# First cross attention: q and k in two 12-bit parts, four products laid over a head's 32 rows, scores in one float32r pass

## The chip, the cores and the metric

The program runs on one core of a Trainium2 chip. TensorE (PE) multiplies matrices and writes only to PSUM; VectorE (DVE), ScalarE (ACT) and GpSimd (POOL) do the elementwise work; SyncE (SP) issues nearly all DMA transfers. The engines run side by side and meet at semaphores. The metric is the device time of one execution in microseconds: the median of three runs of the kernel before is 2702.38 (2698.11 to 2705.56).

## The reference, cut to what matters

Six layers follow each other, each `x = layernorm(x + f(x))`: windowed self attention, cross attention, a mixture of experts, causal self attention, a second cross attention and a ternary feed forward. The change is in the second of them. 64 sequences of 128 tokens of width 128 are handled one by one there:

```
q = (x1 @ Wq + bq)                      # 16 heads of 8 columns
k = concat([x2 @ Wk + bk, memory_k])    # 128 keys from fside, 120 from ctx
v = concat([x2 @ Wv + bv, memory_v])
attn = softmax(einsum('bhqd,bhkd->bhqk', q, k) * D ** -0.5)
out = einsum('bhqk,bhkd->bhqd', attn, v) @ Wp + bp
```

with `x1` the stream, `x2 = fside_BxSxS_0`, and `memory_k = memory_v = ctx_1024`. All of it is float32.

## The kernel before, in words

`attend_keys_major` is the stage. Five engine programs run the same software pipeline, `pipeline(eng, step, ring, nseq, ...)`: `step(c)` is written for a counter c and touches several sequences at different ages (`a = c + 2`, `b = c + 1`, `m = c - 1`, ...), four buffers deep (ring 4); `need(eng, sem, value)` is a wait. The order on each engine is the order in which `step` is written; the middle of the stage is a loop of four steps. There are no planner and no priorities.

A sequence goes this way. SP loads x, ctx and the transposed fside and ctx. TensorE transposes x and projects q, k and v (L1560 to L1562). ScalarE copies q, scaled and with its bias, into `qT` and k into `xf` behind the ctx columns (L1587, L1589), so that the 248 keys of a head lie together. Heads have 8 rows each. The 128 rows of q and k hold 16 heads: 4 row groups of 32 rows, 4 heads in each. GpSimd makes `Qm` (L1732), q four times side by side with all but one head's rows of each 32 set to zero, so that one product over 32 rows gives one head.

Scores are computed twice. "Across" (L1478, L1489), queries on the partitions, 128 x 248 per head, two heads to a PSUM tile, gives VectorE the row maxima (`maxima`, L1625). "Down" (L1473), keys on the partitions, 120 or 128 keys x 4 heads x 128 queries, gets the negated maxima added by a bfloat16 product (L1485, `NB`) and is what ScalarE exponentiates (`exps`, L1577). `scores(c, r)` is one of four rounds of a step: two row groups' down products of an older sequence, mixed with the two other row groups' across products of sequence c. Between the rounds stand `weigh` (L1504, exponents times values), the transposes and the projections. A float32 product appears in the trace as two records, a bfloat16 one as one.

The maxima are split into three bfloat16 parts by GpSimd (L1719 to L1727), turned by TensorE (L1523), and copied by VectorE (L1665). VectorE also does the softmax division, the value bias, and most of the layer norm.

SP's step has seven transfers (L1432, L1433, L1436, L1440, L1444, L1448, L1449), 60 or 64 KB each. They wait for what frees a buffer.

Of the kernel before, what the change touches and what calls it, by code (L numbers as in the profile page):

```python
# [16 lines left out]
F32 = mybir.dt.float32  # L17
BF16 = mybir.dt.bfloat16
U32 = mybir.dt.uint32
# [21 lines left out]
BLANKS = 8  # L41

# [93 lines left out]
def allocate(K):  # L136
# [8 lines left out]
    K.alibi = K.sb("alibi", [P, WH * 48])  # L145
# [7 lines left out]
    K.blank = K.sb("blank", [P, BLANKS, ROW])  # L153
    K.half = K.sb("half", [P, 2])
    K.eps = K.sb("eps", [P, 1])
    K.Mself = K.sb("Mself", [P, WH * P])
    K.Nself = K.sb("Nself", [P, WH * P])
    K.Gram = K.sb("Gram", [P, 2 * P])
# [14 lines left out]
    K.tstep = K.sb("tstep", [P, 3])  # L173

# [84 lines left out]
def late_loads(K, D):  # L259

    return [
        (K.xw[:, 0, :], D["L0_xattn_Wq"]), (K.xw[:, 1, :], D["L0_xattn_Wk"]),
        (K.xw[:, 2, :], D["L0_xattn_Wv"]), (K.xw[:, 3, :], D["L0_xattn_Wp"]),
        (K.xb[:, 0:1], D["L0_xattn_bq"].rearrange("(d a) -> d a", a=1)),
        (K.xb[:, 1:2], D["L0_xattn_bk"].rearrange("(d a) -> d a", a=1)),
# [19 lines left out]
def attend_window(K, D, tag, x_dram, out_dram, nseq):  # L285
# [14 lines left out]
    with ExitStack() as ctx:  # L300
# [53 lines left out]
        with nc.Block() as block:  # L354
            @block.sync
            def _(sp):
# [972 lines left out]
def attend_keys_major(K, D, tag, x_dram, routed, nseq):  # L1329
# [6 lines left out]
    places = (slice(0, CTX), slice(CTX, CTX + P))  # L1336
# [6 lines left out]
    with ExitStack() as ctx:  # L1343
# [3 lines left out]
        def sem(name):  # L1347
# [6 lines left out]
        xf = [sb(f"xf{i}", [P, 2 * P + CTX + P]) for i in range(ring)]  # L1354
        qT = [sb(f"qT{i}", [P, P]) for i in range(2)]
        Qm = [sb(f"Qm{i}", [P, J * P]) for i in range(ring)]
# [24 lines left out]
        f_in = [sem(f"f_in{i}") for i in range(ring)]  # L1381
        xT_out = [sem(f"xT_out{i}") for i in range(ring)]
# [7 lines left out]
        cleared, ready, masked, put_ctx, split, maxed = (sem(n) for n in (  # L1390
            "cleared", "ready", "masked", "put_ctx", "split", "maxed"))
# [6 lines left out]
        cT, kT = slice(2 * P, 2 * P + CTX), slice(2 * P + CTX, 2 * P + CTX + P)  # L1398
        every = slice(2 * P, 2 * P + CTX + P)
# [24 lines left out]
        with nc.Block() as block:  # L1424
            @block.sync
            def _(sp):
                def step(c):
                    a, l, s, o = c + 4, c + 3, c, c - 5
                    if a.live:
                        need(sp, in_sb, (a - 4).done())  # L1430
                        need(sp, put_ctx, (a - 4).done())
                        sp.dma_start(x[a.slot][:], x_dram[a.n]).then_inc(x_in[a.slot], 16)  # L1432
                        sp.dma_start(cx[a.slot][0:CTX, :], D["ctx_1024"][a.n]).then_inc(x_in[a.slot], 16)  # L1433
                    if s.live:
# [21 lines left out]
            def _(pe):  # L1456
# [3 lines left out]
                def scores(c, r):  # L1460
                    t, k, ck, tg, sg, j0 = round_of(c, r)
                    size = sizes[ck]
                    if c.live and r == 0:
                        need(pe, masked, c.done())
                        need(pe, qk_sb, c.done(2))
                    for n in range(2):
                        h = 2 * r + n
                        g, to = tg[n], T[turn[h]]
                        if t.live:
# [3 lines left out]
                            pe.matmul(to[0:size, :], xf[t.slot][rows(g), every][:, places[ck]], Qm[t.slot][rows(g), :],  # L1473
                                      start=True, stop=False)
                        g, to = sg[n], S[turn[h]]
                        if c.live:
                            need(pe, maxed, (c if before[h] < h else c - 1).done(2 * R, before[h] + 1))
                            pe.matmul(to[:, 0:CTX + P], Qm[c.slot][rows(g), P * j0:P * j0 + P],  # L1478
                                      xf[c.slot][rows(g), every], start=True, stop=True)
                    for n in range(2):  # L1480
                        h = 2 * r + n
                        g, to = tg[n], T[turn[h]]
                        if t.live:
                            need(pe, nb_sb, t.done())
# [767 lines left out]
```

## Time and profile before

| | us |
|---|---|
| median of 3 runs | 2702.38 |
| span of the profiled execution (it has no other time of its own) | 2695.8 |
| TensorE busy | 2502.7 (93%) |
| VectorE busy | 1849.6 (69%) |
| ScalarE busy | 1737.7 (64%) |
| GpSimd busy | 1401.1 (52%) |
| first cross attention, its first DMA to its last | 477.84 to about 1124 |
| granted TensorE clock, mean | 0.967 |

The span runs from the first to the last instruction. Busy time is the time in which an engine has at least one instruction in progress; register, semaphore and DMA-issuing instructions do not count. SPq is SP's queue of transfers: its rows give the moment and the length of an issue, not of the transfer. In the waits, an engine's line is followed by what ended its idle time. PEld is the loading of weights, which overlaps with PE.

### The profile page before, as it was taken

The numbers are of one execution on the slowest core, as the hardware profiler recorded it, in microseconds if no ns is written. First come the engines' busy times: TensorE is split into PE (matmuls) and PEld (weight loads), VectorE is DVE, ScalarE is ACT, GpSimd is POOL, SyncE is SP. The second block draws the span as 40 slices with busy tenths as digits, with TensorE's granted clock in tenths as the row PEclk, the third lists the DMA queues.
The fourth block names the chain that finished last, engine by engine and source line by source line (L and its number), as shares of the span: only waits on it lengthen the run. The fifth ranks groups of instructions, "written<-read, shape, count | busy, mean of one in ns | idle before, by whom it ended". The sixth has DMA issues, their size and how long they took to land. (4 is left out here: it accounts for less than half of the span.)

```text
span 2695.8 us, 95989 instructions
## 1 busy us (share of the span) xinstructions
PE 2502.7 (93%) x29950; PEld 2007.2 (74%) x29951; DVE 1849.6 (69%) x5434; ACT 1737.7 (64%) x6375; POOL 1401.1 (52%) x2914
## 2 busy tenths in 40 slices
PE   7999999799999999788889969999999799999995
PEld 6888888577777777487667758888888688888883
DVE  4565555588888888564334448888887388888886
ACT  4666666355555555213556638888888588888883
POOL 2333333233444344165774447777776266666664
PEclk9999999799999999899999979999999899999997
DMA  6332322211111111123332211111111111111100
GB/s 158 100 88 79 89 81 65 65 49 48 49 48 48 48 47 44 37 85 84 78 80 66 66 48 53 47 53 49 50 53 37 33 31 32 31 31 31 31 26 11
DMA packets 270161, 151.37 MB, mean 56 GB/s; under 512 B 51776, under 2 KB 263744, under 8 KB 270016
## 3 DMA queue, kind: packets, MB, share of 16 engines
q1 hardware_dynamic: 261312, 131.57, 18.2%
q0 software_dynamic: 8704, 17.97, 1.9%
q8 instruction: 78, 1.28, 0.2%
q14 instruction: 67, 0.55, 0.1%
HBM read 92.52 MB, written 48.51 MB: 52 GB/s over the span
## 5 line engine op out<-in xcount | busy, mean ns | idle before, releaser
L1187 ACT ACTIVATE pr<-psS,small 128x128 f32<-128x128 f32 x1024 | 366.7, 384 | 95.9 <-DVE small L1258 94.0
L1625 DVE TENSOR_REDUCE small<-psS 128x2 f32<-128x496 f32 x512 | 321.4, 669 | 90.3 <-PE psS L1489 89.1
L1577 ACT ACTIVATE pr<-psT 120x512 f32<-120x512 f32 (+1 forms) x384 | 215.1, 595 | 136.9 <-PE psT L1485 124.5
L1473 PE MATMUL psT<-cross_Qm,cross_xf 32*120 32x512 f32 (+1 forms) x768 | 292.1, 641 | 0.5 <-ACT pr L1577 0.2
L1187 ACT ACTIVATION_READ_ACCUMULATOR pr<-psS,small 128x1 f32 x1024 | 226.1, 221 | 0.0
L1478 PE MATMUL psS<-cross_xf,cross_Qm 32*128 32x248 f32 x1024 | 209.1, 428 | 1.1 <-DVE small L1625 1.1
L2172 POOL DMA_INDIRECT results<-experts_ob,experts_xb x144 | 138.5, 962 | 115.4 <-ACT experts_ob L1992 100.5
L1258 DVE TENSOR_REDUCE small<-psS 128x8 f32<-128x1024 f32 x128 | 156.7, 1224 | 60.5 <-PE psS L1152 60.3
L2112 DVE SCALAR_TENSOR_TENSOR experts_bgh<-experts_bth,psS 128x256 f32<-128x256 f32 x144 | 60.7, 421 | 198.9 <-ACT experts_bth L1984 198.9
L956 POOL TENSOR_SCALAR pr<-pr,small 128x120 f32<-128x120 f32 x512 | 180.4, 372 | 23.3 <-DVE small L910 23.3
L814 ACT ACTIVATE pr<-psS,small 128x120 f32<-128x120 f32 x512 | 179.0, 391 | 5.0 <-DVE small L929 5.0
L1489 PE MATMUL psS<-cross_xf,cross_Qm 32*128 32x248 f32 x1024 | 181.4, 376 | 0.0
L484 ACT ACTIVATE pr<-pr,small 128x48 f32<-128x48 f32 x512 | 166.9, 331 | 2.9 <-DVE small L551 2.9
L1111 PE MATMUL psT<-ident,pr 128*128 128x128 f32 x1024 | 161.6, 281 | 0.2
L1152 PEld LDWEIGHTS psS<-self_qk,self_Qm 32*128 32x128 f32 x2048 | 125.7, 188 | 45.9 <-issue 45.9
L2163 POOL DMA_INDIRECT slots<-routed_x,experts_idx x128 | 123.6, 965 | 66.7 <-issue 38.1
L470 ACT COPY self_Y<-psW 128x512 f32<-128x512 f32 x128 | 68.7, 589 | 126.8 <-PE psW L456 126.8
L1152 PE MATMUL psS<-self_qk,self_Qm 32*128 32x128 f32 x2048 | 150.3, 285 | 0.0
L1473 PE MATMUL psS<-cross_Qm,cross_xf 32*120 32x512 f32 (+1 forms) x256 | 143.9, 642 | 0.0
L1504 PEld LDWEIGHTS psW<-pr,cross_Vx 120*32 120x32 f32 (+1 forms) x4096 | 104.0, 109 | 52.7 <-issue 51.8
L583 POOL TENSOR_TENSOR small<-small,eps 128x1 f32<-128x1 f32 x64 | 12.2, 191 | 249.0 <-DVE small L517 249.0
L1577 ACT ACTIVATE pr<-psS 120x512 f32<-120x512 f32 (+1 forms) x128 | 76.1, 595 | 98.9 <-PE psT L1485 98.9
(323 smaller groups left out, 8058.1 us busy)
## 6 DMA issues: line engine op xcount, KB each, us to landing
self_parts<-results SPq DMA_DIRECT2D x64, 192.0 KB, 2.4
slots<-blank SPq DMA_DIRECT2D x18, 520.0 KB, 4.5
experts_xb<-slots SPq DMA_DIRECT2D x144, 65.0 KB, 1.9
self_near<-in_x SPq DMA_DIRECT2D x128, 64.0 KB, 1.9
between<-self_xo SPq DMA_DIRECT2D x128, 64.0 KB, 1.6
cross_x<-between SPq DMA_DIRECT2D x128, 64.0 KB, 1.8
cross_res<-between SPq DMA_DIRECT2D x128, 64.0 KB, 1.8
self_x<-in_x SPq DMA_DIRECT2D x64, 64.0 KB, 1.8
```

Source lines behind the costliest of these rows:

```text
L484: last = act.activation(head(pr[e.slot], h), head(pr[e.slot], h), ACT.Exp, bias=nmax[e.slot % 2][:, h:h + 1], accum_out=tot[e.slot][:, h:h ...
L814: last = act.activation(pr[b.slot][:, i * P:i * P + CTX], S0[:, i * P:i * P + CTX], ACT.Exp, bias=nmax[b.slot % 2][:, i:i + 1], accum_out= ...
L956: last = pool.tensor_scalar(pr[w.slot][:, i * P:i * P + CTX], pr[w.slot][:, i * P:i * P + CTX], inv[w.slot][:, i:i + 1], 1.0, ALU.mult, AL ...
L1111: last = pe.transpose(W[half][:, n * P:(n + 1) * P], pr[t.slot % 4][:, (4 * half + n) * P:(4 * half + n + 1) * P], K.ident[:])
L1152: last = pe.matmul(K.S[u.slot % 2][:, 512 * half + m * P:512 * half + (m + 1) * P], Qm[i.slot % 2][rows(g), m * P:(m + 1) * P], qk[i.slot] ...
L1187: last = act.activation(pr[e.slot % 4][:, cols], K.S[e.slot % 2][:, cols], ACT.Exp, bias=nmax[e.slot % 4][:, n:n + 1], accum_out=tot[k.slo ...
L1258: dve.tensor_reduce(nmax[u.slot % 4][:], src, AX.X, ALU.max, negate=True).then_inc(maxed, 1)
L1473: pe.matmul(to[0:size, :], xf[t.slot][rows(g), every][:, places[ck]], Qm[t.slot][rows(g), :], start=True, stop=False)
L1478: pe.matmul(to[:, 0:CTX + P], Qm[c.slot][rows(g), P * j0:P * j0 + P], xf[c.slot][rows(g), every], start=True, stop=True)
L1489: pe.matmul(to[:, 256:256 + CTX + P], Qm[c.slot][rows(g), P * j0 + P:P * j0 + 2 * P], xf[c.slot][rows(g), every], start=True, stop=True).t ...
L1577: act.activation(PT[k][0:sizes[ck], 512 * n:512 * n + 512], T[turn[2 * r + n]][0:sizes[ck], :], ACT.Exp).then_inc(exped, 1)
L1625: dve.tensor_reduce(nmax[c.slot % 2][:, J * sg[n] + j0:J * sg[n] + j0 + 2], src, AX.X, ALU.max, negate=True).then_inc(maxed, 1)
```

## The change

Both operands of a score are cut by bits. `high` is the value with its lower 12 bits cleared (VectorE, `bitwise_and` with `0xFFFFF000`), `low` is the value minus `high` (GpSimd); each fits in 12 bits. A score is then four products, high-high, high-low, low-high and low-low, and as a head has only 8 rows, these four take the 32 rows of a row group: row 4d + n of a group holds, for dimension d, product n's part. The two parts of q and k are stored in DRAM (`K.parts`) and loaded back in that layout (`pack`, four heads of 376 columns: 128 of queries, 128 of fside keys, 120 of ctx keys) by six DMAs. For that the columns of Wq, Wk, their biases and a copy of ctx are reordered once outside the kernel (`by_place`). The masked `Qm` goes. Scores are float32r products of `pack` with itself: the down product of 512 columns becomes four of 128, the across product stays at 248 columns. The stage's pipeline is one step longer: projections of q and k run at c + 3, parts are made and stored at c + 2, and `pack` is loaded at c + 1. The value product stays at its old age (now `h = c + 2` in TensorE's step, with its own semaphore `v_ps`), the fside load moves from c + 3 to c + 4.

Some buffers used only by the first stage are given back after it (`early`) to make room, and the first stage's SP now waits for the last blank stores into `slots` (`K.emptied`).

```diff
@@ SP, step of the first cross attention
-                    a, l, s, o = c + 4, c + 3, c, c - 5
+                    a, l, s, o, e, h = c + 4, c + 3, c, c - 5, c + 1, c + 2
+                    if e.live:
+                        need(sp, T_ps, (e - 4).done(2 * R))
+                        need(sp, parts_out[e.slot], e.p * 32 + 32)
+                        for n in range(4):
+                            to = pack[e.slot][n::4, :, :]
+                            of = K.parts[e.slot].rearrange("(j s) h n -> s j h n", j=J)
+                            if n // 2 == n % 2:
+                                sp.dma_start(to, of[:, :, n // 2, :]).then_inc(pack_in[e.slot], 16)
+                            else:
+                                sp.dma_start(to[:, :, queries], of[:, :, n // 2, queries]).then_inc(pack_in[e.slot], 16)
+                                sp.dma_start(to[:, :, keys], of[:, :, n % 2, keys]).then_inc(pack_in[e.slot], 16)
                     if a.live:
...
+                        need(sp, v_ps, (a - 4).done())
+                        sp.dma_start(xf[a.slot][:, P:2 * P], D["t_fside"][a.n]).then_inc(f_in[a.slot], 16)
+                    if l.live:
+                        need(sp, parts_out[(l - 2).slot], (l - 2).p * 32 + 32)
+                        sp.dma_start(low[l.slot % 2][:, 2 * P:], D["t_ctxq"][l.n]).then_inc(c_in[l.slot], 16)
...
-                    if l.live:
-                        need(sp, T_ps, (l - 4).done(2 * R, 4))
-                        sp.dma_start(xf[l.slot][:, P:2 * P], D["t_fside"][l.n]).then_inc(f_in[l.slot], 16)
-                        sp.dma_start(xf[l.slot][:, cT], D["t_ctx"][l.n]).then_inc(f_in[l.slot], 16)
+                    if h.live:
+                        need(sp, low_sb, h.done())
+                        sp.dma_start(K.parts[h.slot][:, 0, :], high[h.slot % 2][:]).then_inc(parts_out[h.slot], 16)
+                        sp.dma_start(K.parts[h.slot][:, 1, :], low[h.slot % 2][:]).then_inc(parts_out[h.slot], 16)
@@ TensorE, one round of scores
-                            pe.matmul(to[0:size, :], xf[t.slot][rows(g), every][:, places[ck]], Qm[t.slot][rows(g), :],
-                                      start=True, stop=False)
+                            pe.matmul(to[0:size, P * j:P * j + P], pack[t.slot][rows(g), j, places[ck]].bitcast(F32R),
+                                      pack[t.slot][rows(g), j, queries].bitcast(F32R), start=(j == 0), stop=False)
...
-                            pe.matmul(to[:, 0:CTX + P], Qm[c.slot][rows(g), P * j0:P * j0 + P],
-                                      xf[c.slot][rows(g), every], start=True, stop=True)
+                            last = pe.matmul(to[:, 256 * j:256 * j + CTX + P], pack[c.slot][rows(g), j0 + j, queries].bitcast(F32R),
+                                             pack[c.slot][rows(g), j0 + j, keys].bitcast(F32R), start=True, stop=True)
@@ TensorE, order in a round: down(j) and across(j) of both row groups
+                        down(n, 0)
...
+                        across(n, 0)
+                    down(0, 1)
+                    down(1, 1)
+                    across(0, 1)
+                    down(0, 2)
+                    down(1, 2)
+                    across(1, 1)
+                    down(0, 3)
+                    down(1, 3)
@@ VectorE, before the first maxima of a step
+                    if h.live:
+                        need(dve, qk_sb, h.done(2))
+                        need(dve, c_in[h.slot], h.landed())
+                        need(dve, parts_out[c.slot], c.p * 32 + 32)
+                        dve.tensor_scalar(high[h.slot % 2][:].bitcast(U32), low[h.slot % 2][:].bitcast(U32), UPPER, None,
+                                          ALU.bitwise_and).then_inc(top_sb, 1)
@@ GpSimd
-                        pool.tensor_tensor(Qm[b.slot][:].rearrange("p (j q) -> p j q", j=J),
-                                           qT[b.slot % 2][:].rearrange("p (j q) -> p j q", j=1).to_broadcast([P, J, P]),
-                                           K.quadmask[:].rearrange("p (j q) -> p j q", q=1).to_broadcast([P, J, P]),
-                                           ALU.mult).then_inc(masked, 1)
+                    if h.live:
+                        need(pool, top_sb, h.done())
+                        pool.tensor_tensor(low[h.slot % 2][:], low[h.slot % 2][:], high[h.slot % 2][:],
+                                           ALU.subtract).then_inc(low_sb, 1)
@@ the stage before, end of SP's program
+                sp.wait_ge(K.emptied, 16 * empty.shape[0])
```

SP's queue, a step of the kernel before, in the fill of the pipeline (the semaphores in brackets are what an instruction waits for):

```order
322 L1448 DMA cross0_xf0<-in_t_fside 128x128 [waits cross0_T_ps]
323 L1449 DMA cross0_xf0<-in_t_ctx 128x120
324 L1432 DMA cross0_x2<-between0 128x128 [waits cross0_put_ctx,cross0_in_sb]
325 L1433 DMA cross0_cx2<-in_ctx_1024 120x128
326 L1436 DMA cross0_res2<-between0 128x128 [waits cross0_joined]
327 L1440 DMA routed_xT<-cross0_xoT0 128x128 [waits cross0_turned_sb]
328 L1444 DMA routed_x<-cross0_xo1 128x128 [waits cross0_normed]
```

The same queue of the changed kernel, from the stores of one step to the middle of the next (`parts` is the DRAM buffer, `pack` the layout of 32-row groups, `high` and `low` the two parts):

```order
396 L1475 DMA parts<-cross0_high0 128x376 [waits cross0_low_sb]
397 L1476 DMA parts<-cross0_low0 128x376
398 L1447 DMA cross0_pack0<-parts 32x4x376 [waits cross0_parts_out0,cross0_T_ps]
399 L1449 DMA cross0_pack0<-parts 32x4x128
400 L1450 DMA cross0_pack0<-parts 32x4x248
401 L1449 DMA cross0_pack0<-parts 32x4x128
402 L1450 DMA cross0_pack0<-parts 32x4x248
403 L1447 DMA cross0_pack0<-parts 32x4x376
404 L1454 DMA cross0_x3<-between0 128x128 [waits cross0_put_ctx,cross0_in_sb]
405 L1455 DMA cross0_cx3<-in_ctx_1024 120x128
406 L1457 DMA cross0_xf3<-in_t_fside 128x128 [waits cross0_v_ps]
407 L1460 DMA cross0_low0<-in_t_ctxq 128x120 [waits cross0_parts_out0]
```

A step of SP goes from 7 transfers to 15: `res`, `routed_xT` and `routed_x` follow as before and then the next two stores. The load in row 398 waits for `parts_out0`, which the stores in rows 396 and 397 raise when they have landed.

TensorE, the last round of a step, before (`psT` and `psS` are the PSUM tiles, `Qm` the masked queries, `xf` the keys):

```order
729 L1473 MATMUL psT<-cross0_Qm2,cross0_xf2 120x512 [waits cross0_exped]
730 L1478 MATMUL psS<-cross0_xf3,cross0_Qm3 128x248 [waits cross0_maxed]
731 L1473 MATMUL psT<-cross0_Qm2,cross0_xf2 120x512 [waits cross0_exped]
732 L1478 MATMUL psS<-cross0_xf3,cross0_Qm3 128x248 [waits cross0_maxed]
733 L1485 MATMUL psT<-cross0_NB0,cross0_onesb 120x512 [waits cross0_nb_sb]
734 L1489 MATMUL psS<-cross0_xf3,cross0_Qm3 128x248
735 L1485 MATMUL psT<-cross0_NB0,cross0_onesb 120x512 [waits cross0_nb_sb]
736 L1489 MATMUL psS<-cross0_xf3,cross0_Qm3 128x248
```

The same round of the changed kernel:

```order
694 L1496 MATMUL psT<-cross0_pack1 120x128 [waits cross0_exped]
695 L1502 MATMUL psS<-cross0_pack2 128x248 [waits cross0_maxed]
696 L1496 MATMUL psT<-cross0_pack1 120x128 [waits cross0_exped]
697 L1502 MATMUL psS<-cross0_pack2 128x248 [waits cross0_maxed]
698 L1496 MATMUL psT<-cross0_pack1 120x128 x2
699 L1502 MATMUL psS<-cross0_pack2 128x248
700 L1496 MATMUL psT<-cross0_pack1 120x128 x2
701 L1502 MATMUL psS<-cross0_pack2 128x248
702 L1496 MATMUL psT<-cross0_pack1 120x128 x2
703 L1529 MATMUL psT<-cross0_NB1,cross0_onesb 120x512 [waits cross0_nb_sb] x2
```

The products of a round go from 8 to 14, with the waits for freed tiles at the same place; the two bfloat16 products now close the round.

## Rows read from the trace of the kernel before

**Rows 1.** First and last start (us) by line: across scores, SP's register operation.
```profile
L1478 PEld LDWEIGHTS psS<-cross_xf,cross_Qm x1024: 181/184/333, 489.5 to 1096.9; 32*128 32x128 f32 x171
...
L1444 SPq FUSED_REGOPS  x52: 46/51/56, 572.0 to 1053.9; - x52
```
**Rows 2.** Busy time by stretch, fill and steady state of the stage.
```profile
core 0: us, PE busy (x) PEld busy (x) DVE busy (x) ACT busy (x) POOL busy (x), PEclk, DMA share, GB/s
470.00:500.00 30.00, 13.54 (x49) 9.12 (x50) 10.73 (x36) 2.05 (x7) 4.92 (x13) 0.55 0.46 111
...
700.00:800.00 100.00, 100.00 (x1474) 70.82 (x1468) 82.25 (x233) 57.80 (x126) 40.64 (x118) 1.00 0.17 49
```
**Rows 3.** Waits of VectorE and ScalarE, 600 to 1070 us: total, times, longest.
```profile
DVE small L1625 <- PE psS L1489: 60.7, 100, 0.9
...
ACT pr L1577 <- PE psT L1485: 169.4, 187, 1.5
```
**Rows 4.** Timeline of TensorE: start, length; rounds and their ends.
```profile
985.58 0.69 PE L1473 MATMUL psT<-cross_Qm,cross_xf 32*128 32x512 f32 x1
...
988.20 0.69 PE L1473 MATMUL psS<-cross_Qm,cross_xf 32*128 32x512 f32 x1
...
989.48 0.33 PE L1531 MATMUL psW<-ident,cross_x 128*128 128x128 f32 x1
...
992.52 0.69 PE L1473 MATMUL psT<-cross_Qm,cross_xf 32*120 32x512 f32 x1
```
**Rows 5.** Timeline of SP's queue: one step of the stage.
```profile
625.14 0.34 SPq L1448 DMA_DIRECT2D cross_xf<-in_t_fside  x1
625.58 0.38 SPq L1449 DMA_DIRECT2D cross_xf<-in_t_ctx  x1
626.20 0.33 SPq L1432 DMA_DIRECT2D cross_x<-between  x1
626.72 0.35 SPq L1433 DMA_DIRECT2D cross_cx<-in_ctx  x1
627.32 0.34 SPq L1436 DMA_DIRECT2D cross_res<-between  x1
627.82 0.49 SPq L1440 DMA_DIRECT2D routed_xT<-cross_xoT  x1
628.46 0.50 SPq L1444 DMA_DIRECT2D routed_x<-cross_xo  x1
634.59 0.34 SPq L1448 DMA_DIRECT2D cross_xf<-in_t_fside  x1
```
**Rows 6.** Waits of SP's queue, 600 to 1070 us.
```profile
SPq L1448 <- PE psT L1485: 263.1, 50, 6.9
```
**Rows 7.** Timeline, later self attention: 16 products with 32-row weights.
```profile
1701.12 1.16 PE L1152 MATMUL psS<-self_qk,self_Qm 32*128 32x128 f32 x16
...
1701.12 0.97 PEld L1152 LDWEIGHTS psS<-self_qk,self_Qm 32*128 32x128 f32 x16 [0.42 <-issue]
```
**Rows 8.** Groups by line, 600 to 1070 us: busy, mean ns.
```profile
L1665 DVE CAST cross_NB<-psW 128x512 bf16<-128x512 f32 x50 | 34.6, 691 | 3.8
L1693 DVE TENSOR_SCALAR cross_xo<-cross_y,small 128x128 f32<-128x128 f32 x50 | 16.8, 337 | 0.0
...
L1732 POOL TENSOR_TENSOR cross_Qm<-cross_qT,quadmask 128x512 f32<-128x512 f32 x50 | 52.1, 1041 | 0.1
L1746 POOL TENSOR_TENSOR cross_yb<-cross_res,rowb 128x128 f32<-128x128 f32 x50 | 22.9, 457 | 0.0
```
**Rows 9.** Timeline of SP's queue, first self attention: loads with a split pattern.
```profile
122.21 0.33 SPq L382 DMA_DIRECT2D self_near<-in_x  x1
122.73 0.33 SPq L383 DMA_DIRECT2D self_near<-in_x  x1
123.15 0.37 SPq L382 DMA_DIRECT2D self_near<-in_x  x1
123.62 0.38 SPq L383 DMA_DIRECT2D self_near<-in_x  x1
```
**Rows 10.** DMA issues: count, KB each, median us from issue to landing.
```profile
self_parts<-results SPq DMA_DIRECT2D x64, 192.0 KB, 2.4
...
between<-self_xo SPq DMA_DIRECT2D x128, 64.0 KB, 1.6
```
**Rows 11.** The stage's start: timeline, and landing of the blank stores.
```profile
473.81 1.62 SPq L389 DMA_DIRECT2D slots<-blank  x2
...
477.84 0.35 SPq L1432 DMA_DIRECT2D cross_x<-between  x1
...
486.15 0.36 ACT L1589 ACTIVATE cross_xf<-psW,xb 128x128 f32<-128x128 f32 x1
...
DMA to landing us min/median/max: 6.7/7.5/8.4
```
**Rows 12.** Down scores and bfloat16 products by line: ns min/median/max, first and last start.
```profile
L1473 PE MATMUL psT<-cross_Qm,cross_xf x768: 587/685/1205, 506.1 to 1111.7; 32*120 32x512 f32 x128, 32*128 32x512 f32 x64
...
L1485 PE MATMUL psT<-cross_NB,cross_onesb x384: 374/374/629, 508.0 to 1112.1; 32*120 32x512 bf16 x128, 32*128 32x512 bf16 x64
```

More of the change, by code:

```diff
@@ L17 @@
 F32 = mybir.dt.float32
+F32R = mybir.dt.float32r
 BF16 = mybir.dt.bfloat16
@@ L173, in allocate @@
     K.tstep = K.sb("tstep", [P, 3])
+    K.alibi = K.sb("alibi", [P, WH * 48], F32, early)
+    K.Mself = K.sb("Mself", [P, WH * P], F32, early)
+    K.Nself = K.sb("Nself", [P, WH * P], F32, early)
+    K.Gram = K.sb("Gram", [P, 2 * P], F32, early)
+    K.blank = K.sb("blank", [P, BLANKS, ROW], F32, early)
 def set_up(K, D):
@@ L1352, in attend_keys_major @@
         res = [sb(f"res{i}", [P, P]) for i in range(ring)]
-        xf = [sb(f"xf{i}", [P, 2 * P + CTX + P]) for i in range(ring)]
-        qT = [sb(f"qT{i}", [P, P]) for i in range(2)]
-        Qm = [sb(f"Qm{i}", [P, J * P]) for i in range(ring)]
+        xf = [sb(f"xf{i}", [P, 2 * P]) for i in range(ring)]
+        low = [sb(f"low{i}", [P, WIDE]) for i in range(2)]
+        high = [sb(f"high{i}", [P, WIDE]) for i in range(2)]
+        pack = [sb(f"pack{i}", [P, J, WIDE]) for i in range(ring)]
         Vx = [sb(f"Vx{i}", [P, 2, G, P]) for i in range(ring)]
@@ L1381, in attend_keys_major @@
         f_in = [sem(f"f_in{i}") for i in range(ring)]
+        c_in = [sem(f"c_in{i}") for i in range(ring)]
+        parts_out = [sem(f"parts_out{i}") for i in range(ring)]
+        pack_in = [sem(f"pack_in{i}") for i in range(ring)]
+        top_sb, low_sb, v_ps = sem("top_sb"), sem("low_sb"), sem("v_ps")
         xT_out = [sem(f"xT_out{i}") for i in range(ring)]
@@ L1389, in attend_keys_major @@
             "in_sb", "qk_sb", "v_sb", "nb_sb", "exped", "O_sb", "oT_sb"))
-        cleared, ready, masked, put_ctx, split, maxed = (sem(n) for n in (
-            "cleared", "ready", "masked", "put_ctx", "split", "maxed"))
+        cleared, ready, put_ctx, split, maxed = (sem(n) for n in (
+            "cleared", "ready", "put_ctx", "split", "maxed"))
         inverted, scaled = sem("inverted"), sem("scaled")
@@ L1553, in step @@
                         need(pe, in_sb, a.done())
-                        need(pe, f_in[a.slot], a.p * 32 + 32)
+                        need(pe, f_in[a.slot], a.landed())
                     if n.live:
@@ L1560, in step @@
                         pe.matmul(W0[:, 0:P], wq, xf[a.slot][:, 0:P], start=True, stop=True)
-                        pe.matmul(W0[:, P:2 * P], wk, xf[a.slot][:, P:2 * P], start=True, stop=True)
-                        pe.matmul(W0[:, 2 * P:3 * P], xf[a.slot][:, P:2 * P], wv, start=True, stop=True).then_inc(proj_ps, 1)
+                        pe.matmul(W0[:, P:2 * P], wk, xf[a.slot][:, P:2 * P], start=True, stop=True).then_inc(proj_ps, 1)
+                    if h.live:
+                        pe.matmul(W0[:, 2 * P:3 * P], xf[h.slot][:, P:2 * P], wv, start=True, stop=True).then_inc(v_ps, 1)
                     if n.live:
```

84 lines of the change are left out of this document (47 added, 37 removed).

## Prediction

> **What bounds the kernel now.** I read the stretch table first, then the timeline of one engine at a time, the waits, and SP's own queue. The change touches one stage, the first cross attention. Its first scores start at 489.5 us and its last score matmul at 1096.9 [rows 1]; SP's register operation that recurs once a step stands 52 times between 572.0 and 1053.9, so a step (one of the 64 sequences) lasts 481.9 / 51 = 9.45 us [rows 1]. In 100 us of it TensorE is busy all the time at a granted clock of 1.00, its 2.4 GHz level, and VectorE 82.25 us [rows 2]: 7.77 us of VectorE work in a step. VectorE waits for TensorE's scores (60.7 us in 470) and ScalarE for TensorE's other scores (169.4 us) [rows 3], and the scores wait for neither. TensorE sets the step; VectorE would be next at about 8 us.
>
> One of the four score rounds of a step starts at 988.20 and the next work begins at 989.48: 1.28 us [rows 4]; the four take about 5.1 of the 9.45. SP issues its seven transfers between 625.14 and 628.96 and sits until 634.59 [rows 5], waiting mostly for the exponents' scores (263.1 us in 50 steps) [rows 6]. It works about 4 us of a step and is never late.
>
> **What the change does to TensorE.** A round had 6 float32 products, two records each (12), and 2 bfloat16 ones; it gets 8 + 4 float32r products and the same 2. If one float32r product is one record of one pass, the weight loads stay 12 + 2 and the columns fall. No row shows float32r. The Trainium skill ("FP8 and Floating Point Precision", TensorE Precision Notes) says a true float32 product takes four passes and a reduced one reads the float32 cut to its upper bits. By that the columns of a round fall from 2 x 512 x 4 + 4 x 248 x 4 + 2 x 512 = 9088 to 8 x 128 + 4 x 248 + 2 x 512 = 3040. The upper bound is no gain: 1.28 us again. Below, the nearest dense row with 32-row weights of 128 columns is the later self attention: 16 such loads in 0.97 us, 0.061 each, and loads and products together about 1.16 [rows 7]. 14 at 0.069 (16 in 1.1) are 0.97 us, which I take: 0.3 us less a round, 1.2 a step. TensorE then needs about 8.2 us.
>
> At that place the skill has a rule against the change: "TensorE: Matmul & The Clock Gate", LDWEIGHTS, gives a load P / 1.2 ns, 107 ns for 128 columns whatever the rows. One after another, 14 would be 1.5 us, longer than the round of now. By the page the step would be 9.45 + 4 x 0.22 = 10.3; by the row it is 8.2. The row decides, since these loads overlap between row groups, but it has two groups in turn and the new round four, so the rule's case stays below as a rival.
>
> **VectorE, ScalarE and GpSimd.** ScalarE has the same two copies as before, into another buffer and one step earlier. VectorE gets one bitwise operation on 128x376. Its neighbours are 0.34 us for 128x128 from SBUF and 0.69 for 128x512 from PSUM [rows 8]; I take 0.5, so VectorE has 7.77 + 0.5 = 8.3 us. GpSimd loses the 1.04 us product of 128x512 and gains a subtraction of 128x376, 0.46 (128x128) to 1.04 [rows 8], say 0.8; it is busy 40 of 100 us [rows 2], so this is free. With some of today's waits left, the compute engines alone would allow a step of about 8.8 (8.3 to 9.2).
>
> **SP's queue, where I expect the end to be set.** All added transfers are SP's: two stores of high and low to DRAM and six loads into pack, beside the seven of before: 15 a step. The listing shows the point: the first pack load waits for `parts_out` of the same item, whose two stores are the two instructions just ahead of it in the queue. SP cannot run ahead of its own stores' landing, once a step, with the whole queue behind it. A step of SP is therefore a plain sum, whatever the other engines do:
> - five gaps between the six pack loads. The self attention issues 32x4x128 loads without a wait between them at gaps of 0.52, 0.42 and 0.47 [rows 9]; five are 0.47 x 3 + 0.43 x 2 = 2.27;
> - last pack load to x (two waits): as 625.58 to 626.20 in the rows, 0.62 to 0.68 over other steps; 0.65;
> - x to cx 0.52, cx to fside 0.6, fside to ctxq 0.52, ctxq to res 0.6, res to xT 0.50, xT to the routed store 0.64, store to the first part 0.6, first to second part 0.44: 4.42, all gaps of the kinds in [rows 5];
> - from the issue of the second store until it has landed. Stores of 64 KB to DRAM land in 1.6 us and loads of 192 KB in 2.4 [rows 10]; mine are 188 KB each, two in flight. Bounds 1.6 and 3.2; I take 2.4, plus 0.1 to wake.
>
> Sum: 2.27 + 0.65 + 4.42 + 2.5 = 9.84, say 9.9 us with the loop's branch. It is above the 8.8 of the compute engines, so SP sets the step and TensorE waits for `pack_in` once a step. Nothing hides it: the landing used to lie beside SP's idle 5.6 us, but only if SP could issue other things meanwhile. The pack loads' own landing (about 2.4) is off this sum, since SP goes on; low is ready long before SP comes to it.
>
> **Fill and drain.** Before: x is asked for at 477.84, ScalarE ends the key copy at 486.5, scores start at 489.5 [rows 11]. Now, behind 486.5: 0.5 (bits), 0.8 (subtraction), 0.45 + 2.5 (stores), 2.3 (six issues), 2.4 (landing) make 495.5: +6. The stage also waits at its start for the last two blank stores, issued from 473.81 and landing after 6.7 to 8.4 us, so until about 482 instead of 477.84 [rows 11]: +4. The drain has shorter rounds: -2. The last step starts at 1096.9 - 6.95 = 1089.95 today, 6.95 being the offset of the fourth round in a step [rows 4]: 600.4 us from the first scores. Then 63 x 9.9 = 623.7.
>
> Change: 10 + 623.7 - 600.4 - 2 = +31 us on a span of 2695.8, so 2727. The median of the runs, 2702.4, is 6.6 us above the span (the profiled execution has no other time of its own): 2733.
>
> **Rivals.**
> - A: the queue is quicker than my sum (landing 1.7, gaps 0.43), SP needs under 8.9, and the compute engines set 8.8. For it: the lower ends of the same rows. Against: those gaps have waits and dynamic addresses between them in [rows 5]. 10 + 554.4 - 602.4 = -38: 2664.
> - B: the sum is 9.4, between the two: 10 + 592.2 - 602.4 = 0: 2702. From there on it is slower; a gain by SP needs under 9.4.
> - C: the weight loads bind TensorE at 10.3 a step: +56, 2759, with SP at 9.9 behind it. For it the page's rule and four row groups; against it the 0.061 of [rows 7].
> - D: TensorE's once-a-step wait (9.9 - 8.2 = 1.7 us) drops the granted clock to 1.2 GHz. At that level a bfloat16 512-column product takes 629 ns instead of 374 and a float32 one 1205 instead of 587 [rows 12]. TensorE's 8.2 us would become some 14: +260. Against: the clock stayed 1.00 wherever waits were this short [rows 2]; only the fill, busy 13.5 of 30 us, shows 0.55 [rows 2].
>
> **Chances.** Forecast (SP's serial sum, 9.6 to 10.5) 0.57; A 0.21; B 0.14; C 0.05; D 0.03. A measurement here tells about 0.3%, 8 us, from no change. Faster by more 0.21, within 0.14, slower 0.65. Landing and gaps put SP's sum between 9.0 and 10.6, which is -33 and +75; the range goes down to A's time, 2664, and up to 2785. D lies outside it.
>
> **What would show it.** If right: SP's first pack load starts 2.4 us behind the second store in every step and SP waits for nothing else; steps of about 9.9; TensorE's largest wait is for the pack load; VectorE busy near 84 of 100 us or less; a round near 1 us with MATMULs of 128 and 248 columns in single records. If SP still has idle time after the routed store, the step is the compute engines' and A holds. Rounds of 1.3 us or more mean the float32r product is no cheaper. It is wrong if the store lands in under 1.9 us or the pack loads issue at under 0.4.

## The result and the profile after

The changed kernel takes 2861.29 us (2854.89 to 2893.28, four runs) against 2702.35 for the kernel before: a ratio of 1.061, 95% interval 1.056 to 1.067. The forecast was 2733, with 2785 as the upper end: the sign was right and the size was not, +159 us instead of +31.

The page of the changed kernel; the rows of digits are the span in 40 slices:

```profile
span 2853.1 us, 96673 instructions
...
PE 2611.3 (92%) x29824; PEld 2124.4 (74%) x29951; DVE 1860.0 (65%) x5498; ACT 1741.2 (61%) x6375; POOL 1395.9 (49%) x2914
...
PEclk9999998575656757657999997999999899999997
```

Slices 8 to 18 are the stage, and there the granted clock is between 0.5 and 0.8; elsewhere it is nearly as it was. All of the loss lies in the stage: the next one starts at 1284.2 us instead of 1126.2 (+158.0) and takes as long as before. A step, from ScalarE's 64 q copies, was (1080.4 - 485.9) / 63 = 9.44 us and is (1214.3 - 492.5) / 63 = 11.46. The fill is longer too: the across scores that began at 489.5 [rows 1] now begin at 503.7.

Durations by line, ns min/median/max, first and last start, against [rows 1, 12]:

```profile
L1496 PE MATMUL psT<-cross_pack x1536: 261/397/472, 516.0 to 1268.1; 32*120 32x128 f32 x128, 32*128 32x128 f32 x64
...
L1502 PE MATMUL psS<-cross_pack x1024: 266/410/763, 503.7 to 1249.3; 32*128 32x248 f32 x171
...
L1529 PE MATMUL psT<-cross_NB,cross_onesb x384: 372/623/646, 516.9 to 1268.3; 32*120 32x512 bf16 x128, 32*128 32x512 bf16 x64
```

1536 records for the 1536 products into `psT`: a float32r product is one record, where a float32 one was two. The bfloat16 product has the same shape as before, and its median went from 374 to 623 ns: more than half of them ran at the low clock level, 1.2 GHz, where [rows 12] has up to 629 for it.

Busy time by stretch, columns as in [rows 2]:

```profile
700.00:800.00 100.00, 95.75 (x1221) 71.78 (x1224) 70.35 (x205) 49.46 (x107) 33.91 (x99) 0.69 0.48 136
800.00:900.00 100.00, 100.00 (x1025) 74.64 (x1017) 58.69 (x169) 41.11 (x88) 27.64 (x83) 0.50 0.44 123
900.00:1000.00 100.00, 93.11 (x1380) 70.21 (x1380) 77.33 (x225) 54.86 (x118) 36.56 (x106) 0.81 0.51 145
```

From 800 to 900 us TensorE has work in progress all the time and is granted 0.50 all the time. ScalarE's q copy comes once a step and tells the pace. Two in a row at the low level, and two at the high level:

```profile
832.23 0.37 ACT L1630 ACTIVATE cross_low<-psW,small 128x128 f32<-128x128 f32 x1 [1.33 <-PE psW L1606]
845.87 0.37 ACT L1630 ACTIVATE cross_low<-psW,small 128x128 f32<-128x128 f32 x1 [1.38 <-PE psW L1606]
...
900.15 0.37 ACT L1630 ACTIVATE cross_low<-psW,small 128x128 f32<-128x128 f32 x1 [1.30 <-PE psW L1606]
908.82 0.37 ACT L1630 ACTIVATE cross_low<-psW,small 128x128 f32<-128x128 f32 x1 [0.32 <-PE psW L1606]
```

A step takes 13.6 us at the low level and 8.7 at the high one. SP's queue at the high level, where [rows 5] had seven issues and idle time:

```profile
903.18 0.43 SPq L1476 DMA_DIRECT2D parts<-cross_low  x1
905.27 0.64 SPq L1447 DMA_DIRECT2D cross_pack<-parts  x1
905.96 0.63 SPq L1449 DMA_DIRECT2D cross_pack<-parts  x1
906.63 0.60 SPq L1450 DMA_DIRECT2D cross_pack<-parts  x1
907.28 0.60 SPq L1449 DMA_DIRECT2D cross_pack<-parts  x1
907.93 0.61 SPq L1450 DMA_DIRECT2D cross_pack<-parts  x1
908.58 0.60 SPq L1447 DMA_DIRECT2D cross_pack<-parts  x1
909.44 0.37 SPq L1454 DMA_DIRECT2D cross_x<-between  x1
...
913.29 0.59 SPq L1475 DMA_DIRECT2D parts<-cross_high  x1
913.92 0.43 SPq L1476 DMA_DIRECT2D parts<-cross_low  x1
915.98 0.64 SPq L1447 DMA_DIRECT2D cross_pack<-parts  x1
```

From first pack load to first pack load, 905.27 to 915.98, is 10.71 us, and nothing else holds SP up: the sum of the prediction's kind, but 10.7 and not 9.9. SP's waits, 600 to 1070 us:

```profile
SPq L1475 <- POOL cross_low L1784: 34.2, 13, 3.0
SPq L82 <- DMA parts<-cross_low: 30.4, 20, 1.6
SPq L1447 <- DMA parts<-cross_low: 17.8, 14, 2.7
```

The stores' landing holds SP 34 times in some 40 steps (L82 is the line of `need`, where a wait stands as an instruction of its own). In the low stretches SP comes early and waits for GpSimd's `low` (34.2 us, 13 times), so there SP isn't the bound. At the high level the other engines step faster than SP, 8.7 us against 10.7: they can, as long as packs are left that SP loaded ahead in the low stretches. TensorE's waits show that it seldom ran out of them, same window:

```profile
PE psW L1572 <- DVE cross_NB L1716: 12.0, 16, 0.9
PE psT L1496 <- DMA cross_pack<-parts: 2.1, 2, 1.2
PEld psT L1496 <- DMA cross_pack<-parts: 1.4, 1, 1.4
```

Three waits for a pack in 470 us, and not one a step as forecast.

So there are two theories for the clock. **Stream**: the products themselves, short float32r ones, keep the clock down. **Wait**: TensorE's waits for the pack bring it down, as the prediction's rival D had it; the three waits above already speak against it. SP's queue is a second cost beside either, wherever the clock stays up.

### The profile page after: what moved, and what is told of

It is laid out like the page before. It is cut to its first block and busy times, and to the rows that moved or that the text cites. A ratio compares the mean times of both kernels' runs of the same rounds, so it can differ in the third digit from the quotient of the medians.

```text
span 2853.1 us, 96673 instructions
## 1 busy us (share of the span) xinstructions
PE 2611.3 (92%) x29824; PEld 2124.4 (74%) x29951; DVE 1860.0 (65%) x5498; ACT 1741.2 (61%) x6375; POOL 1395.9 (49%) x2914
## 3 DMA queue, kind: packets, MB, share of 16 engines
q8 instruction: 78, 1.28, 0.2%
## 5 line engine op out<-in xcount | busy, mean ns | idle before, releaser
L1496 PE MATMUL psT<-cross_pack 32*120 32x128 f32 (+1 forms) x1536 | 241.6, 370 | 4.0 <-DMA cross_pack<-parts 3.5
L1496 PEld LDWEIGHTS psT<-cross_pack 32*120 32x120 f32 (+1 forms) x1536 | 195.8, 264 | 54.6 <-issue 45.2
L1544 PE MATMUL psW<-pr,cross_Vx 120*32 120x128 f32 (+1 forms) x4096 | 208.8, 369 | 0.2 <-ACT pr L1619 0.2
L1544 PEld LDWEIGHTS psW<-pr,cross_Vx 120*32 120x32 f32 (+1 forms) x4096 | 151.1, 147 | 54.8 <-issue 45.6
L1502 PE MATMUL psS<-cross_pack 32*128 32x248 f32 x1024 | 184.9, 431 | 7.6 <-DMA cross_pack<-parts 5.5
L1529 PE MATMUL psT<-cross_NB,cross_onesb 32*120 32x512 bf16 (+1 forms) x384 | 140.3, 542 | 0.0
```

The costliest lines, as they stand in the source:

```text
L1496: pe.matmul(to[0:size, P * j:P * j + P], pack[t.slot][rows(g), j, places[ck]].bitcast(F32R), pack[t.slot][rows(g), j, queries].bitcast(F32 ...
L1502: last = pe.matmul(to[:, 256 * j:256 * j + CTX + P], pack[c.slot][rows(g), j0 + j, queries].bitcast(F32R), pack[c.slot][rows(g), j0 + j, k ...
L1544: last = pe.matmul(W1[rows(g), cols], Vx[t.slot][0:size, ck, g, 32 * j:32 * j + 32], PT[2 * ck + g // 2][0:size, 512 * (g % 2) + P * j:512 ...
```

## The experiments

Steps and stage ends are read from the same places in each trace. "Low" is the time at the 1.2 GHz level between the first q copy and the start of the next stage. A ratio is to the kernel before on the same chip. On the chips of e1, e2, e3 and e11 the kernel before takes about 2815 us, 110 more, all of it in a later stage, so between chips the stage's own columns are to be compared. Rows with an interval were timed several times. e1's four runs took 2932 to 3010 us, and its trace is of one with 2992; its ratio stands as a range. The others were run once.

| run | step | next stage at | low | ratio |
|---|---|---|---|---|
| before | 9.44 | 1126.2 | 35 | 1 |
| after | 11.46 | 1284.2 | 587 | 1.061 [1.056, 1.067] |
| e1_order | 12.22 | 1310.3 | 677 | 1.042 to 1.070 |
| e2_float32 | 10.73 | 1224.6 | 59 | 1.033 |
| e3_f32r_alone | 8.03 | 1032.0 | 39 | 0.967 |
| e3_timed | 8.30 | 1049.0 | 86 | 0.965 [0.963, 0.967] |
| e4_split_alone | 11.84 | 1293.4 | 667 | 1.058 |
| e5_order_float32 | 9.61 | 1151.2 | 45 | 1.006 |
| e6_order_mixed | 9.61 | 1153.8 | 53 | 1.007 |
| e7_wide_down | 10.61 | 1210.5 | 248 | 1.026 |
| e8_order_across32 | 9.61 | 1146.7 | 65 | 1.007 [1.005, 1.009] |
| e9_halves | 8.06 | 1036.6 | 42 | 0.966 |
| e10_order_wide | 9.38 | 1136.7 | 176 | 1.003 |
| e11_stores_on_act | 9.56 | 1141.7 | 66 | 1.003 [1.001, 1.006] |
| e12_zero_parts | 11.35 | 1276.5 | 566 | 1.054 |
| e13_order_zero | 11.53 | 1266.3 | 556 | 1.049 |

### SP's queue and the clock, apart (e1, e2, e5)

e1 is the changed kernel with the new steps of SP in another order, so that other issues stand between the stores and the pack load that needs them:

```diff
                 def step(c):
+                    # loads of x, ctx, fside; then of res
                     if e.live:  # the six pack loads
...
-                    # loads of x, ctx, fside
                     if l.live:  # ctxq
-                    # load of res
```

> The changed kernel with SP's step in another order: x, cx and fside loads first, then the six pack loads, then the rest, the two stores last, so that three other issues lie between the stores and the wait for their landing. SP's own sum is 10.7 us a step in the changed kernel; it should be about 9.1 here. Theory 1 (the float32r rounds are too thin to keep TensorE's clock up, SP's sum is a second and separate cost): the clock still falls for long stretches, a step is 13.3 us in them, and the time stays above 2800. Theory 2 (TensorE's once-a-step wait for the pack loads lets the clock fall): without that wait the clock is 1.0 in the stage, a step 9.1, and the time 2861 - 745 + 63 x 9.1 = about 2690.

The traced run has a step of 12.22 us. The four runs spread too far to say that the new order made it slower (the quickest has a ratio of 1.042, the changed kernel 1.061). The clock fell in all four: their mean over the program is 0.838 to 0.868, where the kernel before has 0.945 to 0.948 on this chip. The wait for the landing was gone, and so was the clock. SP's waits of e1, 700 to 1100 us, and TensorE over 360 us of it:

```profile
SPq L1449 <- POOL cross_yb L1797: 95.8, 29, 3.7
SPq L1475 <- POOL cross_low L1784: 22.6, 27, 1.1
```
```profile
620.00:980.00 360.00, 360.00 (x3706) 268.32 (x3701) 212.82 (x610) 149.15 (x321) 99.30 (x292) 0.50 0.42 118
```

No wait for a landing is left, TensorE waits for no pack from 700 to 1100 us, and the clock is 0.50 for 360 us on end. That speaks against Wait. e2 is the changed kernel with `.bitcast(F32R)` taken off all four operands of the scores:

> The changed kernel with its score products as plain float32 (the bitcast to float32r left out), all transfers and buffers as they are. Theory 1 (thin float32r products): four times the columns bring the clock back to 1.0 over the stage; TensorE needs about 9.5 us a step, SP's 10.7 us sum sets it, TensorE still waits for the pack loads, and the time is about 2861 - 71 = 2790. Theory 2 (the wait for the loads drops the clock): the wait is still there, the clock is mixed again, and as a float32 step at the lower level is about 18 us, the time is 2900 or more.

The same transfers and twice the records for a score product, at the high level throughout. TensorE's waits for the pack, 700 to 1100 us, and its busy time:

```profile
PE psT L1496 <- DMA cross_pack<-parts: 38.8, 36, 1.3
```
```profile
620.00:980.00 360.00, 324.20 (x6199) 255.59 (x6196) 267.00 (x762) 182.23 (x399) 124.04 (x363) 1.00 0.53 148
```

TensorE waits for the pack once a step, 36 times, and keeps 1.00. The step is 10.73 us, SP's 10.7: here the forecast's picture holds, with its sum too small. So the wait is neither needed for the fall (e1) nor enough for it (e2). e5 has both edits, e1's order and e2's float32:

> The reordered SP step (loads of x first, pack loads behind them, stores last) with plain float32 score products. SP's sum: the step of 10.73 us, measured with float32 in the changed order, was SP's alone. Theory (the landing of the stores was serial, and 2.05 - 0.4 us of it now lies beside other issues): the step falls to what TensorE needs, about 9.6 us, clock 1.00, ratio to the kernel before about 1.00 to 1.01. Rival (SP's issues themselves are too many): the step stays above 10.3, ratio above 1.02.

9.61 us. The order alone is worth 1.1 us a step once the clock stays. e2's stage ends 98 us behind that of before (63 x 1.29 = 81 from SP's sum, 17 from the ends), and the changed kernel's ends 60 us behind e2's. These two don't divide the loss into SP's part and the clock's, since the costs hide each other: SP's sum costs nothing in a step of 13.6 us. Without SP's bound the clock costs more: from e5 to e1, each against its own chip's kernel before, it is 100 to 180 us over e1's four runs, and in e4 below it brings the stage's end to 1293.4 with no added transfer at all. 60 us is what the clock adds to a kernel that SP already holds up.

### Which products bring the clock down (e3, e4, e9, e6, e8, e7, e10)

e3 is the kernel before with its score products in float32r and nothing else of the change. For this the keys have buffers of their own, and GpSimd writes the ctx keys once more, rounded to float32r. The scores come from rounded operands, which the changed kernel's two parts avoid:

```diff
-    pe.matmul(to[0:size, :], xf[t.slot][rows(g), every][:, places[ck]], Qm[t.slot][rows(g), :],
+    pe.matmul(to[0:size, :], ky[t.slot][rows(g), every][:, places[ck]].bitcast(F32R), Qm[t.slot][rows(g), :].bitcast(F32R),
```

> The kernel before with only its score products made float32r: masked q and the keys are written rounded to float32r, the ctx keys pass through one more GpSimd operation, no parts, no stores, no pack loads. It computes the scores from rounded operands. Theory 1 (thin products): the clock falls for long stretches although TensorE never waits for a transfer; the stage is no faster than before or slower, 2700 to 2800. Theory 2 (the wait for the loads): no such wait, clock 1.0, a step about 8.1 us as in the changed kernel's best stretch, 2702 - 63 x 1.35 = about 2617.

> The kernel before with its scores' products in float32r alone, as in the run e3_f32r_alone (rounded operands, 512-column down products), timed in rounds this time. Theory 1 (one pass a product at a clock that stays up takes the step to 8.0 us): ratio 0.965 to 0.970, step 8.03, low-clock time under 60 us, as in the single look. Rival: the single look was a lucky one and the clock falls in some executions of it: ratio with an interval that reaches 0.98 or more.

The first run gave a step of 8.03, and timed five times the ratio is 0.965: float32r with 512-column down products is a gain, on both chips. TensorE and VectorE are then equally busy, at about 90% (row of e3_timed):

```profile
900.00:1000.00 100.00, 90.18 (x1363) 64.11 (x1367) 89.20 (x262) 65.96 (x143) 49.30 (x142) 0.95 0.19 53
```

e4 writes e3's round as the changed kernel does: each down product as four of 128 columns, each with its own load of the same weights (14 loads a round for 8), in the changed kernel's order. There is no pack, no store and no new wait.

```diff
-    pe.matmul(to[0:size, :], ky[...][:, places[ck]].bitcast(F32R), Qm[t.slot][rows(g), :].bitcast(F32R), ...)
+    for j in 0..3, interleaved with across:
+    pe.matmul(to[0:size, P * j:P * j + P], ky[...][:, places[ck]].bitcast(F32R), Qm[t.slot][rows(g), P * j:P * j + P].bitcast(F32R), ...)
```

> The kernel before with float32r scores, as in the run with float32r alone, but its round written as in the changed kernel: each 512-column down product as four of 128 columns, same weights loaded four times, 14 weight loads a round instead of 8, same columns. No parts, no stores, no pack loads. Theory 3 (it is the split into short products that lets the clock fall): the granted clock falls to 0.50 for stretches of about 100 us as in the changed kernel, a step is 13 us there and the average of a step goes from 8.03 to 10 or more, the ratio to the kernel before from 0.97 to over 1.02. Rival (the added transfers, or data without zeros, are needed for the fall): clock stays at 0.97 to 1.00, a step 8.1 to 8.5 us, ratio about 0.97.

The same columns and the same numbers multiplied, and the step goes from 8.0 to 11.8 us:

```profile
600.00:700.00 100.00, 100.00 (x1025) 74.55 (x1017) 56.92 (x162) 41.11 (x88) 30.79 (x90) 0.50 0.12 34
```

Beside the changed kernel's 800:900 row it is the same picture, 1025 records at 0.50, with a quarter of the DMA traffic (0.12 against 0.44). This settles it for Stream. e3 and e4 differ less in falling than in coming back: by the clock's records, from 560 us on, e3_timed falls ten times for 3 to 7 us, and e4 three times, for 331, 38 and 246. e9 cuts e3's down product in two of 256 columns instead, in e3's order:

> The run e3_f32r_alone with each 512-column down product as two of 256 columns on the same weights: 10 down and across products a round where it had 8 and the run e4_split_alone had 14, the same columns in all. Theory 1 (the clock falls with the share of TensorE's time that goes to weight loads between short products, by degrees): low-clock time between e3's 39 and e4's 667 us, step 8.1 to 9.5. Theory 2 (only products as short as 128 columns, which leave TensorE no gap, bring it): clock as in e3, under 60 us low, step 8.0 to 8.3.

Clock and step stay as in e3. Between e9 and e4 lie the width, four loads a round and the order, and no run takes these apart. The next two take the changed kernel in e1's order and make only one of the two kinds of product plain float32: in e6 the down products, in e8 the across products.

> The reordered SP step with the down products as plain float32 (128 columns, four passes) and the across products as float32r (248 columns). Theory 3 (short float32r products let the clock fall): with four passes in the short ones the clock stays at 1.00; TensorE needs about 9.0 us a step, SP about 9.3 to 9.7, the ratio to the kernel before is 0.98 to 1.00. Rival (any float32r in this layout lets it fall): low stretches again, ratio over 1.03.

> The changed kernel with the pack and its loads moved ahead in SP's order, the down products float32r (four short ones a round) and the across products plain float32. Every round has 16 down and across products: the four short single-pass ones are there, but the two across products now take four passes. Theory 1 (it is a stream of nothing but short single-pass products that the throttle answers): clock near 1.00, SP or TensorE sets about 9.3 to 9.6 us a step, ratio to before 1.00. Theory 2 (the four short float32r down products bring the fall whatever stands between them): clock near 0.5 to 0.7 in the stage, step 12 or more, ratio 1.06.

Both keep the clock. e8 has all the short float32r down products that the changed kernel has and is at 1.00:

```profile
700.00:800.00 100.00, 93.65 (x1596) 71.15 (x1592) 83.41 (x242) 56.51 (x125) 39.66 (x115) 1.00 0.60 168
```

So in these runs the long low stretches came only where both kinds were float32r and the down ones had 128 columns. e7 and e10 are the changed kernel and e1 with one 512-column down product in place of the four (they leave out the keys of three of a group's four heads):

```diff
-    if t.live:
-        pe.matmul(to[0:size, P * j:P * j + P], pack[t.slot][rows(g), j, places[ck]].bitcast(F32R), ...
+    if t.live and j == 0:
+        pe.matmul(to[0:size, :], pack[t.slot][rows(g), 0, places[ck]].bitcast(F32R), ...
```

> The changed kernel with one float32r down product of 512 columns per row group and chunk in place of four of 128; it leaves out the other three heads' own keys in the down scores. SP's step, stores and loads as in the changed kernel. Theory 3: 8 weight loads a round instead of 14 keep the clock at 1.00 although TensorE waits for the pack loads once a step; a step is SP's 10.73 us, ratio to the kernel before about 1.03. Rival (the wait for the loads together with few columns is enough): stretches at 0.50 remain, the step's mean is over 11 us.

> The changed kernel with the pack and its loads moved ahead in SP's order and its four down products as one of 512 columns (it leaves out the other three heads' own keys). The run e7_wide_down was the same without the new order: step 10.6, 247 us at the low clock. Theory 1 (short products pull the clock, SP's order sets the rest): clock near 1.00 and a step of 9.6 us as in the runs with the new order and float32, set by SP; ratio 1.00 to 1.01. Theory 2 (any float32r scores in this kernel pull the clock once nothing waits on a landing): clock under 0.7 over much of the stage, step 11 or more.

Most of the clock came back, but not all: 0.82 to 0.90, where e3 with the same products had 0.93 or more. No low stretch in them is longer than 14 us from 600 us on, although the products left stand in the changed kernel's order; that speaks against the order as the cause. The steps follow SP's order again (10.61, 9.38). Why these two stay below e3 is open; TensorE is less busy in them, 78 to 88% against e3's 90%.

### Do the numbers matter (e12, e13)

The mask becomes 0 and the lower part is subtracted from itself: all scores are zero, no instruction, transfer or wait changes.

```diff
-    dve.tensor_scalar(high[...].bitcast(U32), low[...].bitcast(U32), UPPER, None,
+    dve.tensor_scalar(high[...].bitcast(U32), low[...].bitcast(U32), 0, None,
-    pool.tensor_tensor(low[h.slot % 2][:], low[h.slot % 2][:], high[h.slot % 2][:],
+    pool.tensor_tensor(low[h.slot % 2][:], low[h.slot % 2][:], low[h.slot % 2][:],
```

> The changed kernel with both parts of q and k made zero (the bit mask is 0 and the lower part is subtracted from itself), so that all scores are zero: each instruction, transfer and wait is left, only the numbers that the score products multiply differ. Theory 1 (the throttle answers to the stream of short single-pass products, whatever they hold): the step is 11.5 and the low-clock time in the stage about 590 us, as in the changed kernel. Theory 2 (it answers to the work that the operands make, which would also explain why the wide products of e7_wide_down lost clock and those of e3_f32r_alone, three quarters zeros, did not): clock near 1.00, step 10.7 set by SP, low-clock time under 100 us, ratio to before about 1.03.

> The run e1_order (the pack and its loads ahead in SP's order) with zero parts as in e12_zero_parts. Theory 1 (the stream alone): step 12 or more, low-clock time about 670 us, ratio about 1.06. Theory 2 (the operands' contents): clock near 1.00 and a step of 9.4 to 9.6 us as in e5_order_float32 or less, ratio about 1.00.

With zeros the clock falls as well. Row of e12:

```profile
800.00:900.00 100.00, 100.00 (x1025) 74.55 (x1015) 58.71 (x169) 41.06 (x88) 26.54 (x83) 0.50 0.42 120
```

e13 is 0.7 us a step better than e1, each from one trace; e1's runs differ by more than that among themselves, so nothing is read from it.

### What holds the reordered kernel at 9.6 us (e11)

e8 with its two output stores issued by ScalarE:

```diff
@@ SP
-    need(sp, turned_sb, z.done()); sp.dma_start(routed.xT[...], xoT[z.slot][:])...
-    need(sp, normed, o.done());    sp.dma_start(routed.x[...], xo[o.slot][:])...
@@ ScalarE, end of a step
+    need(act, turned_sb, z.done()); act.dma_start(routed.xT[...], xoT[z.slot][:])...
+    need(act, normed, f.done());    act.dma_start(routed.x[...], xo[f.slot][:])...
```

> The kernel of the run e8_order_across32 with the two output stores of a step (routed_xT, routed_x) issued from ScalarE's queue instead of SP's. That run had TensorE 94% and VectorE 84% busy at a clock of 1.00 and still a step of 9.55 to 9.6 us; SP's row of issues had no idle gap longer than 0.3 us. Theory 1 (SP's sum of issues is the bound): SP's sum falls by the two stores' 1.2 to 1.4 us to about 8.3, TensorE binds next at 0.94 of 9.55, so a step of 9.0 to 9.1 us; about 32 us off the stage, ratio to before 0.99 to 1.00. Theory 2 (the pack's landing and the DMA queues' share, or the other engines' waits for each other, set the 9.6): step 9.5 or more, ratio 1.00 to 1.01, and ScalarE's share of busy time as before.

Theory 1 fell. SP now has idle time before `res`, once a step, and the step is still 9.56 (the ratio's interval meets e8's):

```profile
904.72 0.40 SPq L1446 DMA_DIRECT2D cross_xf<-in_t_fside  x1
906.76 0.33 SPq L1449 DMA_DIRECT2D cross_res<-between  x1
```

In the reordered kernel SP's sum isn't the bound any more, and what is stays open: TensorE is 94% busy, and some of the rest is its wait for VectorE's `NB`, 20.1 us in 400.

## Why the prediction was wrong, step by step

- **SP's serial sum sets the step: not in this kernel, and its sum was too small by 0.8 us.** It sets the step where the clock stays (e2). In the changed kernel TensorE's low clock sets 13.6 us for long stretches, and TensorE waits for a pack three times in 470 us. SP's sum by its terms: last store to first pack load 2.06 (forecast 2.5); last pack load to x 0.86 (0.65); x to the second store 4.48 (4.42); five pack gaps 3.31 (2.27). The pack gaps carry the error, in part made up by the landing. The pack loads are issued in 0.60 to 0.64 us each, and the rows that the forecast took them from were 0.33 to 0.38 [rows 9]. Even the 32x4x128 pack load takes 0.60, so the transfer's size is not the reason; which part of its pattern is was not tested. Over 63 steps of e2 the 0.83 us are 52.
- **TensorE keeps its clock and needs 8.2 us a step: this step failed.** The sum has no term for the clock. What the runs show in its place: 13.6 us a step at the low level, which held for 587 us of the stage. At the high level steps took 8.4 to 8.7 us with TensorE waiting for VectorE's `NB`, so the 8.2 itself isn't refuted, and the 8.8 forecast for the compute engines was near. Rival D was given 0.03, and with a cause that the runs refute. The prediction counted what a product costs, and not what a stream of such products does to the clock. It also read "the clock stayed 1.00 wherever waits were this short" off rows in which every score was float32, two records each. D's low step of some 14 us was right and its total too high, since the clock recovers between the low stretches: the mean is 11.46. (By the sum that the other rivals use, 14 us a step is +290, not +260; and an SP sum of 9.0 is -25, not the -33 of the range's working.)
- **float32r is one record and a short one: right.** At the high level a round goes from 899.91 to 900.74, 0.83 us (forecast 0.97, before 1.28). The timeline of it, products of the first group first:

```profile
899.91 0.32 PE L1496 MATMUL psT<-cross_pack 32*128 32x128 f32 x1
899.91 0.38 PE L1502 MATMUL psS<-cross_pack 32*128 32x248 f32 x1
...
900.41 0.40 PE L1529 MATMUL psT<-cross_NB,cross_onesb 32*128 32x512 bf16 x2
900.74 1.08 PE L1544 MATMUL psW<-pr,cross_Vx 120*32 120x128 f32 x32
```

- **Rival C, the weight loads: refuted at the high level.** 14 loads and their products fit in 0.83 us. By the Trainium skill's rule ("TensorE: Matmul & The Clock Gate", LDWEIGHTS) they would need 1.5 one after another, an estimate; these 32-row loads in four row groups don't come one after another in the trace.
- **VectorE and GpSimd: right.** The bit operation took 0.35 us (forecast 0.5), the subtraction 0.98 (0.8):

```profile
L1706 DVE TENSOR_SCALAR cross_high<-cross_low x64: 343/345/377, 493.3 to 1215.5; 128x376 uint32<-128x376 uint32 x64
...
L1784 POOL TENSOR_TENSOR cross_low<-cross_low,cross_high x64: 974/984/988, 493.9 to 1216.0; 128x376 f32<-128x376 f32 x64
```

- **Fill +10: measured +14.** SP's first load of the stage starts at 486.10 instead of 477.84, because the blank stores are waited for; the chain from the key copy to the first scores is 10.6 us, 9 forecast. The drain was forecast at -2. From the last q copy to the next stage it is 69.9 us where it was 45.8: +24. e2 shows 14 of them (1165.2 to 1224.6) with the clock no lower than before, 0.91 in both tails, and the pipeline's extra step lies in it; the other 10 come with the low level, 0.50 from 1214 to 1284.

Sum: the stage lost 158 us, against 31 forecast. Either miss alone would have put the time outside the forecast: with the clock kept (e2) the stage ends 98 us later than before, and with the clock lost and no added transfer (e4) 167 later. Together they make 158 and not their sum.

## What to carry to other kernels

Before replacing long or float32 products by many short float32r ones, treat TensorE's clock as something that can be lost: run the new product shapes alone in the old kernel first, as e4 did. A wait on the landing of a store that the same queue has just issued makes that queue a plain sum. Put other issues between the two, and take the issue time of each transfer from a row with its own access pattern, not just its size. Here the part of the change that pays is float32r with wide products: on q and k as they are, unsplit, it gives 0.965 and beats both kernels, at the price of scores from rounded operands.

## What the runs showed of the hardware

A TensorE that is busy without a gap can be held at 1.2 GHz: e1 for 360 us at 100% busy and 0.50, the changed kernel for 100 us at a time. The Trainium skill ("TensorE: Matmul & The Clock Gate", The HAM clock gate) says that idle time brings the low level and sustained activity releases it. e1's 360 us don't agree: work in progress all the time didn't release it. e5 is as busy with float32 products, 99%, and stays at 1.00:

```profile
700.00:800.00 100.00, 99.39 (x1955) 78.25 (x1956) 81.91 (x240) 57.05 (x124) 40.23 (x118) 1.00 0.59 167
```

e2, 90% busy with a wait a step, stays up as well, and e9 (256 columns, 8 down and across products a round) stays up where e4 (128 columns, 12) stays down. (The expectation of e9 counts the two bfloat16 products of a round with them: 10 and 14.) What quantity is watched, these runs don't tell. The same page of the Trainium skill says of another limiter, for a die with three busy cores, that zero operands don't trip it. On this one core zeros changed nothing (e12).
